# Attention step of a three-stage layer kernel: half of the batches moved to the lower rows of TensorE, the next chunk's first layer, the softplus and a scan moved within the step, and the experts' first gathers issued one block later

## What is computed

```python
x = x + 0.5 * ffn(layernorm(x))      # eight experts, top-1 routing, 320 rows each
x = x + attention(layernorm(x))      # a recurrent memory, chunks of 128 rows
x = x + 0.5 * ffn(layernorm(x))
```

```python
g = grad(sum((silu(k @ W1.T) @ W2.T - v) ** 2)) * 0.1      # for each row
g = g * min(1 / norm(g), 1)
S = eta * S - theta * g                                    # scan over the rows
W = (1 - alpha) * W + S                                    # scan over the rows
h = silu(q @ W1t.T); out = h @ W2t.T                       # with the W of the row
out = rmsnorm(out @ Wo.T) * norm_g * (x @ gW.T + gb)
```

## Time and profile before

| | |
|---|---|
| three runs | 846.58 us median (844.75 to 847.06) |
| profiled execution | 846.02 us, of which the span of instructions is 844.2 us |
| PE busy (matmuls) | 720.9 us, 85% of the span |
| DVE, ACT, POOL busy | 591.8, 439.1 and 248.4 us (70%, 52%, 29%) |
| mean granted clock of PE | 0.907 |

### The profile page before, as it was taken

The page is one execution under the profiler, slowest core; times in us unless marked ns, Lnnn a source line. Parts: engine busy times, 40 slices in busy tenths (PEclk is TensorE's granted clock), DMA queues, the critical chain, the costliest instruction groups (busy, mean ns, idle before and its releaser), DMA issues. The chain is left out here.

```text
span 844.2 us, 15540 instructions
## 1 busy us (share of the span) xinstructions
PE 720.9 (85%) x5702; PEld 632.8 (75%) x5702; DVE 591.8 (70%) x1300; ACT 439.1 (52%) x1040; POOL 248.4 (29%) x184
## 2 busy tenths in 40 slices
PE   5439999996868989899899999999877238999996
PEld 2139999996657878788788888878766128899996
DVE  0867777743688678888787977876753756877861
ACT  1506547541554586665866568576432505565650
POOL 0044511314123062350613515151232045512202
PEclk9859999998997999999898998999969658999999
DMA  8966723604101012130221303103030732616300
GB/s 341 415 237 206 270 86 146 206 17 132 50 0 51 2 60 92 40 111 2 90 62 50 100 2 106 46 1 101 1 88 15 248 101 92 217 52 225 118 14 32
DMA packets 57858, 89.19 MB, mean 106 GB/s; under 512 B 6592, under 2 KB 48704, under 8 KB 57664
## 3 DMA queue, kind: packets, MB, share of 16 engines
q1 hardware_dynamic: 45808, 70.18, 23.9%
q0 software_dynamic: 3840, 10.49, 3.7%
q10 hardware_dynamic: 8144, 7.61, 2.9%
HBM read 74.63 MB, written 22.02 MB: 114 GB/s over the span
## 5 line engine op out<-in xcount | busy, mean ns | idle before, releaser
L626 PE MATMUL ps<-moe_normedT_high,weights_high_up 128*128 128x320 f32 x256 | 85.3, 333 | 4.8 <-DVE moe_normedT_low L456 3.8
L627 PE MATMUL ps<-moe_normedT_low,weights_high_up 128*128 128x320 f32 x256 | 82.9, 324 | 0.0
L628 PE MATMUL ps<-moe_normedT_high,weights_low_up 128*128 128x320 f32 x256 | 82.9, 324 | 0.0
L484 DVE SCALAR_TENSOR_TENSOR moe_hidden_low<-ps,moe_hidden_high 128x256 fp32r<-128x256 f32 x128 | 53.9, 421 | 37.3 <-ACT moe_hidden_high L589 32.9
L1087 POOL TENSOR_TENSOR att_o_rs<-att_o_mean,minus_half 128x4 f32<-128x4 f32 x16 | 16.2, 1013 | 210.3 <-DVE att_o_mean L1326 210.3
L626 PE MATMUL ps<-weights_high_down,moe_hidden_high 128*128 128x256 f32 x256 | 73.4, 287 | 0.0
L628 PE MATMUL ps<-weights_high_down,moe_hidden_low 128*128 128x256 f32 x256 | 71.5, 279 | 0.0
L627 PE MATMUL ps<-weights_low_down,moe_hidden_high 128*128 128x256 f32 x256 | 71.4, 279 | 0.0
L567 ACT CAST weights_high_down<-weights_raw_down 128x256 fp32r<-128x256 f32 x96 | 35.0, 406 | 41.6 <-PE ps L628 34.1
L626 PEld LDWEIGHTS ps<-moe_normedT_high,weights_high_up 128*128 128x128 f32 x256 | 51.4, 201 | 6.8 <-DVE moe_normedT_low L456 4.4
L588 ACT ACTIVATE moe_shared<-ps 128x64 f32<-128x64 f32 x128 | 28.9, 226 | 48.3 <-PE ps L628 43.2
(11 more groups left out here) (298 smaller groups left out, 2138.2 us busy)
## 6 DMA issues: line engine op xcount, KB each, us to landing
weights_raw_up<-in_w SPq DMA_DIRECT2D x16, 1024.0 KB, 9.9
weights_raw_down<-in_w SPq DMA_DIRECT2D x16, 1024.0 KB, 8.9
first_xt<-in_xT SPq DMA_DIRECT2D x8, 1024.0 KB, 7.7
weights_rows<-x SPq DMA_DIRECT2D x8, 1024.0 KB, 5.6
out_x<-weights_rows SPq DMA_DIRECT2D x8, 1024.0 KB, 4.4
weights_rows<-x ACTq DMA_DIRECT2D x7, 1024.0 KB, 5.4
weights_rows<-x SPq DMA_DIRECT2D x2, 512.0 KB, 4.3
weights_raw_up<-in_w_x SPq DMA_DIRECT2D x1, 704.0 KB
```

What stands on the lines that cost most here:

```text
L484: v.scalar_tensor_tensor(hidden_low[i][:, f, :], ps[:, 2 + (KF * i + f) % 3, WHOLE[i]], 0.0, hidden_high[i][:, f, :].bitcast(F32), ALU.max ...
L626: mm(dst, high_l, high_r, start=start, stop=False)
L627: mm(dst, high_l, low_r, start=False, stop=False)
L628: return mm(dst, low_l, high_r, start=False, stop=stop)
```

## The change

1. Batches 4 to 7 keep their keys, first-layer weights and hidden values in partitions 64 to 127. `SIDES` names the two halves, and `IN_TURN` is the order 0, 4, 1, 5, ... in which `score`, `hidden` and `second_scores` go through the batches, so that products of the upper and of the lower rows alternate. Each half writes to its own bank of the PSUM pair. Many operations of ACT, DVE and POOL that touched one half of the partitions for eight batches are now two operations for four batches each. The hidden values are turned by seven transposes of two batches each instead of eight.
2. PE does `hidden(c + 1)` in mid-step, between `second_scores` and the gates, and ACT's Silu and Tanh of it follow there. The logits' products wait for them, since they share C.
3. ACT does `thetas(c)` one step later, behind the gradients' squares and the copy of the keys' projection.
4. DVE does `decay_scans(c + 1)` behind `key_norms` instead of behind `ends`, and POOL does `residual(c, 0)` ahead of `prep(c + 1)`.
5. The first chunk's preamble is reordered on DVE in the same sense: the scans of carry and AB come last.
6. `weights.gather(0)` is the first work of POOL in the experts block, not the last of the route block. `first_low` is gone; its 16 pieces are made in the experts block, five of them ahead of pair 0 and the others in `beside_up`.

```diff
 # experts
+            weights.gather(0)
             power_of(0, slice(0, FIRST))
...
             def beside_up(g, i, f, first, last):
-                if first and i == 0 and f < KF - 3:
-                    low_piece(g, DOWN[0], f + 3)
-                if i == 0:
+                if first and i == 0:
+                    if f + EARLY < KF:
+                        low_piece(g, UP[0], f + EARLY)
+                    low_piece(g, UP[1], f)
+                    low_piece(g, DOWN[0], f)
+                elif first or i == 0:
                     low_piece(g, DOWN[1], f)
-                elif not last:
+                if i == 1 and not last:
                     low_piece(g + 1, UP[0], f)
 # attention
+    UPPER, LOWER = slice(0, D), slice(D, P)
+    SIDES = (slice(0, HALF), UPPER, LOWER), (slice(HALF, B), LOWER, UPPER)
+    IN_TURN = [(h * HALF + b, SIDES[h][1]) for b in range(HALF) for h in range(2)]
...
 # POOL, step
                 output_power(c, 0)
+                residual(c, par, 0)
                 if not last:
                     prep(c + 1, False)
-                residual(c, par, 0)
                 output_power(c, 1)
 # DVE, step
                     ends(c + 1, 1 - par, first)
-                    decay_scans(c + 1)
                 output_mean(c, 0)
...
                     key_norms(c + 1, 1 - par)
+                    decay_scans(c + 1)
                 gated_output(c, par, 0)
 # ACT, step
-                    gradients(c)
+                gradients(c)
                 if not last:
                     kv_projection(c + 1)
+                thetas(c, par, first)
                 if not first:
                     result_turned(c - 1, 0)
...
                     new_gram(c + 1)
+                    hidden(c + 1, False)
...
-                    thetas(c + 1, 1 - par, False)
                     keys(c + 1, False, final)
-                    hidden(c + 1, False)
 # PE
-                for b in range(B):
-                    last = mm(wide(C)[:, b, 0:D], KV[par][0:D, b, :], state[par][0:D, b, 0:D], start=True, stop=True)
+                for b, rows in IN_TURN:
+                    last = mm(wide(C)[:, b, 0:D], KV[par][rows, b, :], state[par][rows, b, D:2 * D], start=True, stop=True)
...
                 gram(c + 1)
-                if not first:
-                    logit_products(c - 1)
                 second_scores(c, par)
+                hidden(c + 1, 1 - par, False, first)
+                gates(c + 1, (0, ))
+                if not first:
+                    pe.wait_ge(hid_ready, c + 2)
+                    pe.wait_ge(bend_ready, c + 2)
+                    logit_products(c - 1)
+                gates(c + 1, (1, ))
+                retrieve(c, par)
                 if not first:
                     logit_turn(c - 1)
-                gates(c + 1, (0, 1))
-                retrieve(c, par)
                 gates(c + 1, (2, 3))
                 outputs(c, 0)
                 keys(c + 1, 1 - par)
                 queries(c + 1, 1 - par)
-                hidden(c + 1, 1 - par, False)
```

More of the change, by code:

```diff
@@ L1060, in setup @@
             def setup():
-                g.memset(carry[0:D, :, :], 0.0).then_inc(folded, 1)
-                g.memset(state[0][D:P, :, :], 0.0).then_inc(folded, 1)
+                for n, own, other in SIDES:
+                    g.memset(carry[own, n, :], 0.0)
+                    g.memset(state[0][other, n, :], 0.0).then_inc(folded, 1)
                 pool.wait_ge(folded, 7)
@@ L1345, in step @@
                     split_turned(c + 1)
-                if not first:
+                if first:
+                    decay_scans(c)
+                else:
                     slope_of(c)
@@ L1363, in step @@
                 second_scores(c, par)
-                if not first:
+                if last:
                     logits(c - 1)
@@ L1503, in keys @@
                     act.wait_ge(grad_w1_ready, c)
-                s.activation((first_k_sq if first else k_sq)[:], wide(BB)[:, :, 0:D], ACT.Square).then_inc(k_squared, 1)
+                for n, own, _ in SIDES:
+                    last = s.activation((first_k_sq if first else k_sq)[:, n, :], wide(BB)[:, n, own], ACT.Square)
+                last.then_inc(k_squared, 1)
             def hidden(c, first):
@@ L1515, in hidden_turned @@
                 act.wait_ge(hid_turned, c + 1)
-                s.copy(KV[par][0:D, :, :], wide(C)[0:D, :, :]).then_inc(hid_turned_copied, 1)
+                for n, own, _ in SIDES:
+                    last = s.copy(KV[par][own, n, :], wide(C)[own, 1:HALF + 1, :] if own is UPPER else wide(C)[own, n, :])
+                last.then_inc(hid_turned_copied, 1)
                 if not first:
@@ L1596, in step @@
                     normalise(c + 2)
+                if not first and not last:
+                    logits(c - 1)
                 retrieve(c)
@@ L1725, in queries, with hidden @@
                 score(par, A)
-            def hidden(c, par, first):
+            def hidden(c, par, first, second=False):
                 pe.wait_ge(kv_conv, TAPS * c + TAPS)
@@ L1742, in hidden_turned @@
                 pe.wait_ge(bend_ready, c + 1)
-                for b in range(B):
-                    last = nc.tensor.transpose(wide(C)[0:D, b, :], hid[:, b, :], t["ident"][:])
+                if not first:
+                    pe.wait_ge(lg_read, c)
+                for b in range(1, B):
+                    last = nc.tensor.transpose(wide(C)[:, b, :], hid[:, b - 1:b + 1, :].rearrange("p b n -> p (b n)"),
+                                               t["ident"][:])
                 last.then_inc(hid_turned, 1)
@@ L1768, in second_scores @@
                 pe.wait_ge(hid2_ready, c + 1)
-                for b in range(B):
-                    last = mm(wide(DD)[:, b, :], KV[par][0:D, b, :], hid2[0:D, b, :], start=True, stop=True)
+                for b, rows in IN_TURN:
+                    last = mm(wide(DD)[:, b, :], KV[par][rows, b, :], hid2[rows, b, :], start=True, stop=True)
                 last.then_inc(hh_made, 1)
@@ L1804, in gram @@
                 pe.wait_ge(w2_copied, n + 1)
-                for b in range(B):
-                    w2 = read_w[D:P, b, D:P]
-                    last = mm(C[0:D, 0, b * D:(b + 1) * D], w2, w2, start=True, stop=True)
+                for n, own, other in SIDES:
+                    for b in range(n.start, n.stop):
+                        w2 = read_w[other, b, D:P]
+                        last = mm(C[own, 0, b * D:(b + 1) * D], w2, w2, start=True, stop=True)
                 last.then_inc(gram_made, 1)
```

159 lines of the change are left out of this document (89 added, 70 removed).

## The result

The changed kernel takes 885.07 us (881.52 to 887.12, four runs) against 846.82; the ratio is 1.045, with a 95% interval of 1.041 to 1.049. It is slower, as forecast, but by 38 us where 6 to 7 were forecast, and it lies 20 us above the upper end of the range.

The account below looks back on a forecast made before the run. It took DVE's gated output to pace each attention step's first half, PE the rest, and POOL to become late. 846.0 + 15 (six steps) + 0.3 (last chunk) − 4 (first chunk) − 4.1 (experts) = 853 us; range 833 to 865.

Parts of the forecast that it names:

- What set the first half before: Old attention step, first half: PE waits, and DVE's second gated output sets the result's first turn, at T0 + 18.6 on average.
- The bound of the new step, and POOL's lateness: New first half: POOL becomes late, its power delays the second gated output to T0 + 19.7 against 18.6, +1.1 us.
- The middle of the step: Summing the new step: 19.7 + 19.4 (turn to rates' end) + 14.8 (to next T0) = 53.9 us against 51.5.
- a rival with a chance of 0.17: PE's clock falls once more in each step, or the softplus delays the turned result's copy: 862 us, chance 0.17.
- 3.2 + 1.1: Mid-step: first layer waits until 3.2 us after the rates for ACT's copy of the gram, then takes 1.1.
- The first layer in mid-step: Moving it is worth nothing in the first half; rates' end to next T0 grows by 1.3 to 14.8 us.
- DVE's order: First half: KNORM no longer waits, AB scan ends at T0 + 8.4, first gated output at T0 + 10.0.
- Softplus: Moved to the next step's first half, on ACT: cost to PE's second turn taken as nothing, bounds 0 and 2.9 us.
- Alternation: Alternating halves on PE: a group of eight products takes 1.1 us instead of 1.9, 0.8 less at three places.
- First chunk: Reordered scans of carry and AB on DVE: −4 us, bounds 0 and −5.
- Experts: Gathers and low pieces moved: −0.8 us in the first pass, −3.3 in the second, together −4.1, bounds 0 and −7.
- slower still: Rival: clock falls once more per step, or the turned result's copy is late; 1.6 us a step, 862 us, chance 0.17.

Follow-up runs that it names:

- run 1: Changed kernel with POOL making QAB and MIX ahead of the first residual again; 883.09 us, 1.040 times the kernel before.
- Fill_both: Changed kernel plus 16 unread products ahead of the result's first turn and six ahead of the first layer in mid-step; 874.19 us, 1.035 times the kernel before.
- runs 3: Changed kernel with the first layer, its Silu and Tanh back at the step's end and the logits' products in their old places; 871.08 us, 1.025.
- run 9: Kernel of run 6 plus the next chunk's first layer, and ACT's part of it, in mid-step; 855.98 us, 1.012 times the kernel before.
- prep_first: Same run as run 1: changed kernel with POOL's QAB and MIX ahead of the first residual again; 883.09 us, 1.040.
- hid_scan: Changed kernel with first layer, AB scan and POOL's order put back, softplus left behind the gradients' squares; 854.90 us, 1.010 times the kernel before.
- run 2: Changed kernel plus 16 unread products on PE ahead of the first turn of the result; 879.92 us, 1.035 times the kernel before.
- halves_natural: Kernel of run 6 with score, first layer and second scores going through batches 0 to 7 in order; 835.73 us, 0.990 times the kernel before.
- halves_turn: Kernel of run 6 with the turn of the logits behind the first pair of gates; 834.11 us, 0.990 times the kernel before.
- run 4: Changed kernel with first layer, softplus, AB scan and POOL's order undone; halves, first chunk's order and experts' part left; 839.21 us, 0.987 times the kernel before.
- run 6: Kernel of run 4 with the experts and route blocks of the kernel before; 839.74 us, 0.990 times the kernel before.
- run 7: Same run as hid_scan: changed kernel with only the softplus's move left within the step; 854.90 us, 1.010.
- run 5: Kernel before with the experts' part of the change alone (gathers first in the experts block, low pieces moved); 849.77 us, 1.003.
- Fill_turn: Same run as run 2: changed kernel plus 16 unread products ahead of the result's first turn; 879.92 us, 1.035.

## Why the prediction was wrong, point by point

**What set the first half before: in part misread.** The prediction says that PE waits in the first half, and that DVE's gated output sets the turn. In the step that it shows, PE is busy for 17.58 of the 18.14 us up to the turn, and its last product ahead of it ends at 467.19, between the end of the gated output, 467.11, and the turn, 467.25:

```profile
466.80 0.39 PE L1655 MATMUL ps<-att_xT_high,att_w_low 128*128 128x512 f32 x1
```

In all six steps PE comes to the turn without a wait. So PE, with a stretch at half clock of its own, and DVE were through at the same time; nor is there thin work ahead of that stretch in this step, PE is busy for all of the 5.5 us before it. In the changed kernel PE is through at T0 + 15.6 in four of the six steps, and DVE and POOL at 20.5. The gap between them is where the clock then falls.

**The bound of the new step, and POOL's lateness: right in kind.** POOL's power follows MIX with no idle time and the second gated output waits for it, as forecast. That output ends at T0 + 20.5 instead of 19.7. The term was mis-sized by 0.8: QAB takes 2.92 instead of 2.36, and MIX's pieces 1.08 and three times 0.62 instead of 0.53 each, while the chain starts 0.3 earlier. That POOL's order alone is not the cause is shown by run 1.

**The middle of the step: the step that failed.** The sum took "19.4" from the old trace for turn to rates, and 14.8 for rates to T0, both at full clock, although the prediction itself had found 2 to 3.6 us of idleness ahead of the first. It priced the clock only in a rival with a chance of 0.17 and at 1.7 us a step. Fill_both measures it: 3.7 us a step, 22 us in all, 2.2 behind the turn and 1.5 on average behind the first layer's wait. The second of these waits stood in the sum as 3.2 + 1.1, but nothing was made of it for the clock. The same working with 3.7 us a step would have given 853 + 22 = 875. The profiled execution took 886.6. The other 11 to 12 us are POOL's 0.8 and mid-step's 0.5 at full clock, together 8 in six steps, and 7 in the first chunk, less some 4 in the last chunk and the experts.

**The first layer in mid-step: right within 0.5 at full clock, 15.3 against 14.8.** That the first half would gain nothing from its leaving is shown by runs 3 and 9.

**DVE's order: right in its times.** The AB scan ends at T0 + 8.1 (8.4), the first gated output at T0 + 9.7 (10.0), KNORM no longer waits. Its price was not seen: prep_first and hid_scan split the first half from 16.5 with both orders put back to 19.1 with the scan late, and to 20.5 with POOL's order too.

**Softplus: right in the six steps.** The second turn does not wait there in the changed kernel, and run 2 shows no loss by it. It does in hid_scan, 2.87 us, close to the bound of 2.9 that was given for that case. What the softplus costs in the first chunk was not in the sum.

**Alternation: right in size, wrong in worth.** A group of scores or second scores takes 1.16 us for 16 instructions (1.1 forecast; 1.9 to 2.05 before). The sum gave it 0.8 in mid-step; halves_natural and halves_turn show 0, because waits for ACT and then for DVE stand behind it.

**First chunk: wrong sign in the changed kernel, +3.3 instead of -4.** Its preamble does gain: without the moves the first chunk is 6.2 us shorter (run 4, and 62.5 us in run 6). Most of what takes this back is the softplus: with it alone moved the chunk takes 70.3 us (run 7), with the first layer alone moved 63.1 (run 9), and with all moves 72.2. The prediction named the softplus here, but gave its new place no price; in the changed kernel DVE waits 5.26 us for it in the first chunk, and PE 3.0 us for the gradients behind it:

```profile
261.46 0.69 DVE L1271 SCALAR_TENSOR_TENSOR att_theta_log<-att_GATES,att_theta_log 128x512 f32<-128x512 f32 x1 [5.26 <-ACT att_theta_log L1520]
```

**Experts: wrong, nothing that can be told instead of -4.1 (run 5).** The entries gained more than forecast: DVE's first norm starts 3.5 us earlier in the first pass instead of 1.8, at 51.43, since DVE begins when the first gather has landed and not the third, and in the second pass it starts 25.6 us after the end of the attention instead of 34.1, 8.5 less where 4.3 were forecast. The products then take longer. From the first `up` to the last `down`, the first block takes 138.6 to 148.9 us in the eight profiled executions with the experts' part of the change, and 136.6 to 142.8 in the six without it; the second block takes 138.8 to 145.7 and 133.9 to 141.3. In one of the traces where the first is long, that of prep_first, ACT waits 10.6 us for the load of a `down` weight, and DVE 2.9 us for ACT behind it. That the moved low pieces make these loads late is argued, not shown.

The rivals: "slower still" was the right mechanism with the wrong price. Its 862 was too low, because it counted one fall of the clock where there were two, and because the first chunk, POOL and mid-step were off as well.

## What to carry to other kernels

A wait of PE is priced twice: by its length, and by what the dense work behind it takes if the clock falls. Where a reordering leaves PE idle ahead of dense work, put the fall into the sum itself, for each such wait, with the bounds that traces show: here 1.5 us of waiting were followed by no fall in some steps and by up to 3.1 us of loss in others. Unread products in the gap are a cheap test of it: they add work and free no other engine, so what they give back is the clock's.

Before an engine's saved time is counted, ask who is ready behind it. Here PE's 0.8 us from alternation went first to ACT, then to DVE. And before an operation is moved in the loop, ask what its new place does in the first pass: the softplus cost the first chunk 7.6 us.

## What the runs showed of the hardware

**DVE and POOL hold each other up.** In the rows above DVE's L1302, with both inputs in SBUF, takes 2.75 us beside POOL's L1050, while the same form just before it takes 0.68; in the kernel before, and in run 4, it took 0.69 in all eight chunks, with nothing on POOL. It ends 0.55 us after QAB does. In all six steps it was 2.75 to 2.78, in prep_first, beside the last of MIX and the residual, 1.0. The Trainium skill ("SBUF — State Buffer", section "Who interferes with whom") says that an operation of VectorE with two inputs in SBUF and one of GpSimd that reads SBUF exclude each other for a whole instruction, whoever is first; these rows agree, and so do QAB's 2.92 us, as it starts together with L1300 (2.35 in prep_first), and the 1.08 us of MIX's first piece, which starts while L1302 is not yet done (0.62 for the next). The 2 us were hidden behind POOL's own lateness here, but the mean that the power needs stood behind them.

**A product with useless results can be worth more than a wait.** Fill_turn has 16 more products a step and is 2.4 us a step shorter.

**Products of the two halves follow each other faster when they alternate.** 16 loads of 64 rows and 128 columns with their 16 products take 1.16 us when the halves alternate and 1.71 with four batches of one half and then four of the other (2.05 in one half alone, before): 72, 107 and 128 ns for a load and its product. A load's own record is 188 ns in all three, so what overlaps more is not to be read from the records, only that the spacing is shorter. The load time that the Trainium skill gives for 128 columns, 107 ns whatever the rows ("TensorE: Matmul & The Clock Gate", section on LDWEIGHTS), is the spacing of the second case; the first shows that it is no floor for the spacing when the rows of neighbours differ.
